# Queries and keys split into 16-bit halves in token order and turned by DMA, in an attention and feed-forward kernel

## What is computed

```python
xn = layernorm(x)                          # (32, 256, 128)
q, k, v = split(rmsnorm(xn) @ [Wq, Wkv])   # 16 heads of 64
q, k = head_rmsnorm(q), head_rmsnorm(k)    # q / max(|q|, 1e-12) * (gamma + 1) * 8
sim = tanh(q @ k.T / 50) * 50 / 8
attn = softmax(sim) @ v @ Wo
h = gelu(xn @ (W1 + scale * m1(xn)).T + b1)        # m1, m2: products of 16 token rows of the batch
out = x + attn + h @ (W2 + scale * m2(xn)).T + b2
```

## Time and profile before

| | |
|---|---|
| Time, median of 3 runs | 1260.57 us (1260.56 to 1261.61) |
| The profiled execution's own time | 1261.8 us |
| Its span, first to last instruction | 1259.8 us |
| Busy: PE, PEld, DVE, ACT, POOL | 93%, 77%, 82%, 86%, 73% |
| Mean granted TensorE clock | 0.992 |

### The profile page before, as it was taken

The page is one execution under the profiler, slowest core; times in us unless marked ns, Lnnn a source line. Parts: engine busy times, 40 slices in busy tenths (PEclk is TensorE's granted clock), DMA queues, the critical chain, the costliest instruction groups (busy, mean ns, idle before and its releaser), DMA issues.

```text
span 1259.8 us, 36165 instructions
## 1 busy us (share of the span) xinstructions
PE 1165.6 (93%) x13897; PEld 972.3 (77%) x13897; DVE 1032.2 (82%) x2153; ACT 1082.2 (86%) x2055; POOL 917.6 (73%) x1105
## 2 busy tenths in 40 slices
PE   3789999999999999999999999999999999999988
PEld 2468887778877778878778878778878778878777
DVE  6788889888889888889888889888889888888862
ACT  3589898889898889888888988888988888988885
POOL 4477777777777777877777877777777777777663
PEclk9899999999999999999999999999999999999999
DMA  4000000000000000000000000000000000000000
GB/s 132 10 11 11 14 16 7 15 15 11 15 15 7 15 15 11 15 15 7 15 15 11 14 16 7 15 15 11 14 15 7 15 15 15 10 11 11 11 6 9
DMA packets 32224, 19.41 MB, mean 15 GB/s; under 512 B 3508, under 2 KB 31288, under 8 KB 32056
## 3 DMA queue, kind: packets, MB, share of 16 engines
q1 hardware_dynamic: 32056, 17.12, 4.7%
HBM read 12.13 MB, written 4.19 MB: 13 GB/s over the span
## 4 chain that ended last, share of the span: by engine, by line
PE 42%; DVE 25%; ACT 19%; issue 11%; POOL 1%; ACTq 0%; POOLq 0%
PE ps_scores L481 8%; ACT probs L563 6%; PE ps_aux L455 5%; DVE qk L729 4%; PE ps_aux L448 4%; PE ps_aux L406 4%; PE ps_y L525 4%; DVE heads_T L738 3%; DVE sel_rows L760 3%; DVE qk L694 3%; PE ps_aux L408 3%; PE ps_aux L407 3%; ACT L596 3%; DVE norm L667 3%; ACT hid L596 3%
## 5 line engine op out<-in xcount | busy, mean ns | idle before, releaser
L905 POOL TENSOR_TENSOR probs_lo<-probs 128x512 f16<-128x512 f32 x512 | 586.3, 1150 | 235.1 <-ACT probs L563 232.9
L555 ACT ACTIVATE clamped<-ps_scores 128x512 f32<-128x512 f32 x512 | 310.3, 606 | 124.5 <-PE ps_scores L481 124.4
L563 ACT ACTIVATE probs<-clamped 128x512 f32<-128x512 f32 x512 | 324.9, 635 | 0.4
L503 PE MATMUL ps_o<-v_hi,probs 128*128 128x65 bf16 x2048 | 240.0, 195 | 4.5 <-DVE o_sb L706 2.7
L504 PE MATMUL ps_o<-v_lo,probs 128*128 128x64 bf16 x2048 | 239.2, 193 | 0.0
L505 PE MATMUL ps_o<-v_hi,probs_lo 128*128 128x65 bf16 x2048 | 238.9, 194 | 0.0
L481 PE MATMUL ps_scores<-heads_T 64*128 64x256 f16 x3072 | 212.9, 271 | 14.2 <-ACT clamped L555 14.0
L406 PE MATMUL ps_aux<-w_hi,xhT_hi 128*128 128x512 f32 x384 | 191.5, 499 | 31.9 <-DVE qk L729 21.6
L503 PEld LDWEIGHTS ps_o<-v_hi,probs 128*128 128x128 bf16 x2048 | 192.1, 99 | 30.1 <-issue 18.2
L504 PEld LDWEIGHTS ps_o<-v_lo,probs 128*128 128x128 bf16 x2048 | 189.8, 99 | 5.0
L505 PEld LDWEIGHTS ps_o<-v_hi,probs_lo 128*128 128x128 f16 x2048 | 190.2, 98 | 0.0
(11 more groups left out here) (83 smaller groups left out, 2211.2 us busy)
## 6 DMA issues: line engine op xcount, KB each, us to landing
x_in<-in_L_attn_tokens_dram SPq DMA_DIRECT2D x32, 128.0 KB, 2.3
x_res<-in_L_attn_tokens_dram SPq DMA_DIRECT2D x32, 128.0 KB, 2.3
out_dram<-y_sb SPq DMA_DIRECT2D x32, 128.0 KB, 1.9
sel_raw<-xn SPq DMA_DIRECT2D x192, 4.0 KB
qk<-in_L_attn_Wkv_dram SPq DMA_DIRECT2D x2, 512.0 KB, 5.4
qk<-in_L_attn_Wq_dram SPq DMA_DIRECT2D x1, 512.0 KB, 3.6
qk<-in_L_ffn_W_dram SPq DMA_DIRECT2D x2, 256.0 KB
hid<-in_L_attn_q_gamma_dram SPq DMA_DIRECT2D x1, 512.0 KB, 7.0
```

The costliest lines, as they stand in the source:

```text
L503: pe.matmul(full, hi[:, col], v_hi[:, par, u, h], start=(u == 0), stop=False)
L555: nc.scalar.activation(clamped[:, buf], ps_scores[:, s % SCORE_BANKS], ACT.Tanh).then_inc(clamp_done, 1)
L563: nc.scalar.activation(probs[:, buf], clamped[:, buf], ACT.Exp, bias=LIFT, scale=SOFTCLAMP * DH ** -0.5).then_inc(probs_done, 1)
L905: g.tensor_tensor(probs_lo[:, buf], probs[:, buf], probs[:, buf].bitcast(BF16)[:, 1::2], ALU.subtract).then_inc(lo_made, 1)
```

## The change

The eight `qkT` products, their bank uses, their copies and their subtractions go. In their place, for each chunk of four heads, ACT rounds the normalised `qk` to 16 bits as it stands (128x1024 from SBUF to the new buffer `halves16`), DVE subtracts to get the low part (`halves`), and SP starts two DMAs with transposition (`turn_heads`), 256 KB each, one for the high and one for the low part, into `heads_T`. `halves16` has two places, so that ACT's copy for a chunk waits for the DMAs of the chunk two before. The scores of each second pair wait for the DMAs (`heads_turned`). All tables are written anew: products in other slots, `xhT` and `xnT` joined into one `xT` in slot 11, and `norm_stats` moved from slot 1 to slot 8 of DVE, `rstd` from slot 1 to slot 10 of POOL, the choice of rows (`select`) from slot 14 to slots 3 and 4.

```diff
+    (1, "q", 2, 1), (1, "q", 3, 1),
+    (2, "oT", 0, -1), (2, "oT", 1, -1),
+    (3, "k", 2, 1), (3, "k", 3, 1),
+    (4, "oT", 2, -1),
+    (5, "v", 0, 1), (5, "v", 1, 1),
+    (6, "oT", 3, -1), (6, "low", 0, 0),
+    (7, "v", 2, 1), (7, "v", 3, 1),
     (9, "hid", 0, 0), (9, "hid", 1, 0),
+    (10, "low", 1, 0),
+    (11, "xT", 0, 2),
+    (13, "q", 0, 2), (13, "q", 1, 2),
+    (15, "k", 0, 2), (15, "k", 1, 2),
...
+    [("divide",), ("sum", 5), ("select_rows",)],
...
+    [("norm_stats",)],
     [("divide",), ("norm_apply",)],
...
+    [("lo",), ("rstd",)],
...
+HALF_STEPS = {0: (3, 0), 11: (0, 1), 12: (1, 1), 14: (2, 1)}
+TURN_STEPS = {3: (3, 0), 12: (0, 1), 13: (1, 1), 15: (2, 1)}
...
+Y_PRODUCTS = {4: 4, 6: 4, 8: 4, 10: 3, 11: 2, 12: 4, 14: 3}
...
+        halves16 = sb("halves16", [P, 2, 2, PAIRS // CHUNKS, TT * 2, P], F16)
+        heads_T = sb("heads_T", [P, 2, PAIRS, TT, 2, P], F16)
...
+            def turn_heads(st, c, ahead):
+
+                b, _, _ = st.batch(ahead)
+                wait(sp, scores_done, HEADS * (b - 1) + 4 * c + 4)
+                for half, made in enumerate((half_hi_made, half_lo_made)):
+                    sp.wait_ge(made, CHUNKS * b + c + 1)
+                    sp.dma_start(heads_T[:, half, 2 * c:2 * c + 2].rearrange("p a t j n -> p (a t j) n"),
+                                 halves16[:, c % 2, half].rearrange("p a b n -> p (a b n)"),
+                                 transpose=True).then_inc(heads_turned[c], 16)
...
-                wait(pe, qkT_split, PAIRS * b + pair + 1)
+                if pair % 2 == 0:
+                    wait(pe, heads_turned[pair // 2], 32 * (b + 1))
...
+                    if s in HALF_STEPS and STAGE[HALF_STEPS[s][1]] in st.stages:
+                        c, ahead = HALF_STEPS[s]
+                        b, par, _ = st.batch(ahead)
+                        act.wait_ge(qk_normed, CHUNKS * b + c + 1)
+                        wait(act, heads_turned[(c + 2) % CHUNKS], 32 * (b + c // 2))
+                        nc.scalar.copy(halves16[:, c % 2, 0], chunk_of(par, c)).then_inc(half_hi_made, 1)
...
+            def halves(st, c, ahead):
+
+                b, par, _ = st.batch(ahead)
+                dve.wait_ge(half_hi_made, CHUNKS * b + c + 1)
+                v.tensor_tensor(halves16[:, c % 2, 1], chunk_of(par, c), halves16[:, c % 2, 0], ALU.subtract)\
+                    .then_inc(half_lo_made, 1)
```

More of the change, by code:

```diff
@@ L79 @@
 VECTOR_STEPS = [
-    [("result",), ("sum", 0)],
-    [("norm_stats",), ("sum", 1), ("divide",), ("splits",)],
-    [("splits",)],
-    [("divide",), ("sum", 2), ("splits",)],
-    [("sum", 3), ("sum", 4), ("normalise", 3, 0)],
-    [("divide",), ("updates",), ("sum", 5), ("splits",)],
-    [("sum", 6), ("splits",)],
-    [("sum", 7), ("seed",), ("divide",), ("splits",)],
-    [("splits",)],
-    [("divide",), ("norm_apply",)],
-    [("updates",), ("splits",), ("normalise", 0, 1)],
-    [("splits",), ("divide",), ("normalise", 1, 1)],
-    [("splits",)],
-    [("divide",), ("normalise", 2, 1)],
-    [("splits",), ("select",)],
-    [("splits",), ("divide",)],
+    [("result",), ("normalise", 3, 0)],
+    [("divide",), ("splits",), ("sum", 0)],
+    [("sum", 1), ("halves", 3, 0), ("sum", 4)],
+    [("divide",), ("sum", 5), ("select_rows",)],
+    [("select_low",), ("sum", 2), ("sum", 3)],
+    [("divide",), ("splits",)],
+    [("updates",), ("sum", 6), ("sum", 7), ("seed",)],
+    [("divide",), ("splits",)],
+    [("norm_stats",)],
+    [("divide",), ("norm_apply",)],
+    [("normalise", 0, 1), ("updates",)],
+    [("divide",), ("splits",), ("halves", 0, 1)],
+    [("normalise", 1, 1), ("halves", 1, 1)],
+    [("divide",), ("splits",)],
+    [("normalise", 2, 1), ("halves", 2, 1)],
+    [("divide",)],
 ]
 POOL_STEPS = [
-    [("lo",)],
-    [("lo",), ("rstd",)],
     [("lo",), ("square", 0)],
     [("lo",), ("square", 1)],
-    [("lo",), ("bias",)],
+    [("lo",)],
+    [("lo",)],
     [("lo",), ("square", 2)],
     [("lo",), ("square", 3)],
+    [("lo",)],
     [("lo",), ("newton", 0)],
@@ L423, in aux @@
                 done = aux_filled[kind]
-                if kind in ("xhT", "xnT"):
+                if kind == "xT":
                     wait(pe, xn_made, b + 1)
                     for t in range(TT):
-                        ins = pe.transpose(bank[:, t * P:(t + 1) * P], xh[:, t] if kind == "xhT" else xn[:, par, t],
-                                           ident[:])
+                        pe.transpose(bank[:, t * P:(t + 1) * P], xh[:, t], ident[:])
+                    for t in range(TT):
+                        ins = pe.transpose(bank[:, seq + t * P:seq + (t + 1) * P], xn[:, par, t], ident[:])
                 elif kind in ("q", "k"):
@@ L440, in aux @@
                     ins = mm3(bank, xhT_hi[:, par, tok], xhT_lo[:, par, tok], w_hi[:, col], w_lo[:, col])
-                elif kind == "qkT":
-                    if k % 2 == 0:
-                        wait(pe, qk_normed, 4 * b + k // 2 + 1)
-                    for j in range(2):
-                        for t in range(TT):
-                            at = j * HEADS * DH + k * P
-                            ins = pe.transpose(bank[:, (j * TT + t) * P:(j * TT + t + 1) * P],
-                                               qk[:, par, t, at:at + P], ident[:])
                 elif kind == "oT":
@@ L481, in scores @@
                             ins = pe.matmul(ps_scores[:, odd, t * seq:(t + 1) * seq],
-                                            heads_T[rows, pair, left, k, keys], heads_T[rows, pair, right, q],
+                                            heads_T[rows, left, pair, t, k], heads_T[rows, right, pair, :, q],
                                             start=(i == 0), stop=(i == 2))
@@ L748, in aux, with select_rows @@
                         .then_inc(weff_made, 1)
-            def select(st):
-                b, _, _ = st.batch(1)
+            def select_rows(st):
+                b, _, _ = st.batch(0)
                 dve.wait_ge(rows_loaded, 16 * 6 * (b + 1))
@@ L797, in run @@
                             result(st)
-                        elif what == "select" and "front" in st.stages:
-                            select(st)
+                        elif what == "select_rows" and "attn" in st.stages:
+                            select_rows(st)
+                        elif what == "select_low" and "attn" in st.stages:
+                            select_low(st)
                         elif what == "sum" and "front" in st.stages:
@@ L804, in run @@
                             rsqrt_seed(st)
+                        elif what == "halves" and STAGE[k[1]] in st.stages:
+                            halves(st, *k)
                         elif what == "normalise" and STAGE[k[1]] in st.stages:
```

70 lines of the change are left out of this document (28 added, 42 removed), and 6 rows, old and new, of the table AUX.

## The result

The changed kernel takes 1454.32 us (median of 4 runs, 1453.84 to 1454.79), the kernel before 1261.09 us beside it (4 runs, 1260.56 to 1263.57): a ratio of 1.153 (95% interval 1.151 to 1.155), 193 us slower. The prediction said 1430, in a range of 1250 to 1540.

A forecast was written before the change was run, and what follows sets the result against it. PE and ACT close the old 37.7 us loop; the late normalisation chain, with DVE's order behind it, makes it 43.4. 1260.6 + 171 (30 x 5.7) - 3 (last two steps) gives about 1430 us, range 1250 to 1540.

The forecast's parts named there:

- 1. `rstd` ends: From tanh 9's end (t = 0): exponential 9 on ACT, `lo` 9 and `rstd` on POOL to 8.0; `norm_apply` to 10.0.
- 2. `halves` 1 end: DVE behind `norm_apply`: chunk 0's work and `normalise` 1 to 14.9, then ACT's rounding and `halves` 1 to 17.2.
- Step 3: DVE: divide, two q splits, `normalise` 2 to 20.0; ACT's rounding and `halves` 2 to 22.3; `normalise` 3 to 24.3.
- step 4: ACT squares slot 1's q products by 27.0; DVE's splits, sums, `halves` 3 and row choice follow, `v` 0 split at 37.2.
- step 5: PE's `low` 0, output, values and scores to 41.7; ACT's tanh 8, exponential and tanh 9 to 43.4.
- The wait for `rstd`: DVE stands ahead of `norm_apply` for POOL's `rstd` once a batch, 6 to 7.5 us, some 200 us in all.
- The round trips: DVE waits twice a batch, about 1.1 us each, at `halves` 1 and 2 for ACT's rounding of a just normalised chunk.
- `halves` of 128x1024: DVE's new subtraction, taken at 1.13 us like `normalise`; the upper bound was `w_lo` at 1.70 us.
- ACT's waits: ACT waits about 3 to 4 us a batch for PE's turn of `xT`, about 1.3 us for `normalise` at chunks 1 and 2.
- Nobody waits for a DMA: Transposing DMAs of 256 KB cost nothing: 3.3 us each, two in a row 6.6, inside a cover of 7.7.
- The rival from the Trainium skill: Transposing DMAs far slower than plain: eight blocks in a row 10.5 us, 84 us a batch, some 2650 us; chance 0.12.
- The faster rival: DVE's work after `norm_apply` is absorbed, only the shortest loop counts: 36.5 us a batch, 1225 us; chance 0.12.

The follow-up runs named there:

- e1: Changed kernel with `norm_stats` back in DVE's slot 1 and `rstd` back in POOL's slot 3, all else as changed: 1354.83 us, ratio 1.073.
- e2: Kernel before the change with only `norm_stats` moved to DVE's slot 8 and `rstd` to POOL's slot 10: 1414.08 us, ratio 1.120.
- e3: Changed kernel with `rstd` one slot earlier on POOL, at the end of slot 9, ahead of `lo` 9: 1398.96 us, ratio 1.108.
- e7: Changed kernel with each chunk normalised at least a slot before its `halves`, `norm_stats` and `rstd` left late: 1408.26 us, ratio 1.115.
- e4_pe_filler: Changed kernel with 24 unread 128x512 matmuls on PE ahead of its wait for the normalised input (`xh`): 1470.45 us, ratio 1.165.
- e12_after_short_lo: Changed kernel with POOL's `lo` of heads 9 to 13 cut to 64 of 512 columns, the rest left out: 1411.91 us, ratio 1.118.
- e9_newton_early: Kernel of e5_roundtrip with POOL's third Newton step right behind the second, ahead of `lo` 9: 1254.17 us, ratio 0.993.
- e5_roundtrip: Changed kernel with `norm_stats` and `rstd` back early and each chunk normalised at least a slot before its `halves`: 1257.07 us, ratio 0.996.
- e11_short_lo: Kernel of e9_newton_early with POOL's `lo` of heads 9 to 13 cut to 64 of 512 columns, the rest left out: 1218.94 us, ratio 0.966.

## Why the prediction was right, step by step

The cause and the size held. The five steps, in the prediction's own clock (t = 0 is 644.19 in the trace of the changed kernel; as in the prediction, an instruction in DVE's full queue is taken to end where the next one starts, only the split of `v` 0 at its own end):

| step | forecast t | measured t |
|---|---|---|
| 1. `rstd` ends | 8.0 | 7.9 |
| `norm_apply` ends | 10.0 | 10.1 |
| 2. `halves` 1 end | 17.2 | 17.7 |
| 3. `halves` 2 end | 22.3 | 22.9 |
| `normalise` 3 ends | 24.3 | 25.0 |
| 4. split of `v` 0 ends | 37.2 | 38.2 |
| 5. next tanh 9 ends | 43.4 | 44.1 |

- **The wait for `rstd`**, 6 to 7.5 us a batch and some 200 in all: 6.7 and 204.3. Shown as the main cause by e1, e2, e3 and e7: put back, it gives 99.5 us, and made late in the kernel before it takes 151.
- **The missing 24 us** (1454.3 against 1430): from tanh 9 to tanh 9, 30 turns take 1322.9 us against 1130.2 before, 6.4 us more a turn where 5.7 were forecast, which is 21 us. The other 3 are in the filling: the first tanh 9 ends 2.5 us later (71.2 against 68.7), which the sum had at nothing. The gain of 3 us that was forecast for the last two steps is there: the last turn is 0.5 us shorter than before, and what follows it 2.5.
- **The 0.7 us a turn**: 0.5 of them are there at `halves` 1, and 0.3 of these are PE's low clock, by which ACT gets the turned `xT` later (e4_pe_filler). The prediction had no term for the clock. Step 3 adds 0.2 us, step 4 adds 0.3, and step 5 gives 0.3 back. e12_after_short_lo shows that the two `xn` take 0.73 us longer beside `lo` 10. The prediction took `norm_apply` at the 2.0 us of the earlier trace rows, where a `lo` of POOL (635.86 to 636.90) also stood beside it, so its sum holds most of this without having named it.
- **The round trips** of 1.1 us: two a batch, as written; with a third of 0.22 us ahead of `halves` 0 they make 79.6 us in 97 times. That they are worth 97.8 us once the chain is early, and only half of that beside the late chain, was not forecast.
- **`halves` of 128x1024**: 1239 ns at 1.14 from start to start, forecast 1.13 by `normalise` rather than 1.70 by `w_lo`. This was right for this kernel only: in e9_newton_early the mean is 1691. The two ends of that range seem to be the same kind of operation with POOL out of its way and in it: each of the three `w_lo` of 1.70 us stood beside instructions of POOL that make `mask`.
- **ACT's waits**: for the turn of `xT` 3 to 4 us forecast, 4.64 measured. Part of the difference is PE at half clock: its four transposes take 1.1 us there and 0.7 in e4_pe_filler. For `normalise`, about 1.3 us were forecast at chunks 1 and 2; the step shown has no such wait at chunk 1, 0.91 us at chunk 2 and 0.31 at chunk 3.
- **Nobody waits for a DMA**: right. Each was forecast at 3.3 and landed in 3.2, between the plain ones of the earlier trace rows, which agrees with the Trainium skill, "Advanced Engine Details and Errata", "X-Bar Transpose (TRN2)". The rival from the Trainium skill, "VectorE: DVE Perf Modes", "The three transpose paths", read as eight blocks of 1309 ns one after another, is contradicted by the 3.2 us for eight blocks: its figure cannot be the price of each block in a row of them. The two of a pair overlap and land in 4.4 us, not in 6.6 one after the other, so that the cover is 3.1 us where the prediction's 7.7 - 6.6 would give 1.1.
- **The faster rival** (1225, only the shortest loop counts) is out: DVE's work behind `norm_apply` is not absorbed. Even with both waits gone the kernel stands at 1254; DVE is then busy for 1127.0 us of 1252.7.
- **Where the relief of PE went**: in e5_roundtrip PE is busy 1072.9 us, 93 less than before, for no time at all in the steady turns. DVE is busy 1098.8 us, 67 more than the 1032.2 of the earlier trace rows; `halves` and `normalise` alone take 73 us more than in the changed kernel (389.2 against 316.0), beside POOL's instructions. e11_short_lo, which takes some of that away, falls at once to 1219. That DVE is the bound is argued from this; what binds at 1219 stays open.

The trace agrees with the Trainium skill, "SBUF — State Buffer", "SBUF: two separate sides": the pair of ports that VectorE and GpSimd share is held for a whole instruction by whichever starts first, and a VectorE operation with two inputs in SBUF has to wait for a GpSimd operation that reads SBUF. Over all `halves` of e9_newton_early, those that started with 900 ns or more of a POOL instruction still to run took a median of 2056 ns (61 of them), those that found POOL idle 1208 ns (32).

## What to carry to other kernels

An instruction moved to a later slot costs what stands *ahead of it in its engine's order* at the new place, not what it waits for itself: `rstd` needs four numbers that were ready 6 us before, and came late because POOL had `lo` 8, two `newton` steps and `lo` 9 ahead of it, the last of which waited for an exponential. When an engine hands work to another and takes it back, put a slot of other work between the two, and give the engine that frees a bank its split first. "Nobody waits for it" says that a transfer or an operation is hidden now, not by how much: measure the cover before spending it, and if two engines both read SBUF with two inputs, look at each duration beside what the other was doing when it started.
